# A decoder layer on one core: where TensorE waits for each part of an operand, three moved copies and transfers, and a shorter last offset

## The reference

```python
x = layernorm(x + attention(x))    # 32 query heads, 8 key/value heads of 128, causal, window 128
x = layernorm(x + cross(x, ctx))   # matmul(fake_quant(x), fake_quant(ctx)), 8 bits
x = layernorm(x + ffn(x))          # ternary weights, hidden size 2752
# attention: q, k, v = x @ wq.T, x @ wk.T, x @ wv.T; p = softmax(mask(q @ k.T / sqrt(128)))
#            (p @ v) @ wo.T, everything in fp32
# fake_quant(a): (clip(round(a / s + z), 0, 255) - z) * s
# ffn(x): gate, up = x / 128 @ wg.T, x / 128 @ wu.T; i = trunc(clip(silu(gate) * up * 128, -128, 127))
#         trunc(clip(i @ wd.T * 128, -128, 127)), as int8
# layernorm: (x - mean) / sqrt(var + 1e-5)
```

## Time and profile before

| | |
|---|---|
| median of 3 executions | 1465.61 us (1465.59 to 1466.85) |
| the profiled execution, its own time | 1466.88 us |
| its span in the trace | 1465.1 us |
| PE busy | 1429.0 us, 98% of the span |
| DVE, ACT, POOL busy | 68%, 53%, 51% |
| moved by DMA | 283.20 MB, 193 GB/s on the mean |
| mean granted clock of TensorE | 0.996 |

### The profile page before, as it was taken

One profiled execution on the slowest core, in us unless ns is written; L12 is line 12 of the kernel. 1 busy time (PEld: TensorE's weight loads), 2 busy tenths in 40 slices (PEclk: granted clock), 3 DMA queues, 4 the chain that ended last, 5 costly groups with the idle time before them and its releaser, 6 DMA issues.

```text
span 1465.1 us, 22782 instructions
## 1 busy us (share of the span) xinstructions
PE 1429.0 (98%) x7024; PEld 1153.3 (79%) x7024; DVE 999.4 (68%) x1768; ACT 782.7 (53%) x1553; POOL 740.7 (51%) x651
## 2 busy tenths in 40 slices
PE   8899999999999999999999999999989999999997
PEld 6688888888888888888888888887657888778643
DVE  7644444445656578888888888887786656566597
ACT  5433333333345466666575666565466555555674
POOL 0477777777565454555455555554476333433100
PEclk9999999999999999999999999999999999999998
DMA  6477877776663757675757676763151222222611
GB/s 230 146 271 283 286 281 270 273 275 256 212 239 108 282 180 277 200 267 179 265 196 271 206 265 209 269 236 127 41 181 74 94 100 81 76 93 86 230 43 74
DMA packets 114330, 283.20 MB, mean 193 GB/s; under 512 B 21216, under 2 KB 21600, under 8 KB 114272
## 3 DMA queue, kind: packets, MB, share of 16 engines
q1 hardware_dynamic: 114272, 282.50, 55.1%
HBM read 184.94 MB, written 95.42 MB: 191 GB/s over the span
## 4 chain that ended last, share of the span: by engine, by line
PE 50%; DVE 7%; ACT 4%; DMA 3%; issue 3%; POOL 2%; SPq 0%; DVEq 0%; ACTq 0%; POOLq 0%
PE ps L1141 7%; PE ps L1143 7%; PE ps L1142 7%; PE ps L1297 6%; PE ps L1298 5%; PE ps L1350 5%; PE ps L1070 2%; PE ps L1071 2%; PE ps L1072 2%; PE ps L1118 2%; PE ps L1117 1%; PE ps L1119 1%; PE ps L1083 1%; DVE u_val L2853 1%; PE ps L1222 1%
## 5 line engine op out<-in xcount | busy, mean ns | idle before, releaser
L1051 PE MATMUL ps<-xo_h,wb_h 128*128 128x512 f32 x644 | 251.6, 391 | 5.2 <-DVE xo_l L2391 2.0
L1053 PE MATMUL ps<-xo_h,wb_l 128*128 128x512 f32 x644 | 250.7, 389 | 0.0
L1052 PE MATMUL ps<-xo_l,wb_h 128*128 128x512 f32 x644 | 250.6, 389 | 0.0
L1141 PE MATMUL ps<-wo_h,o_h 128*128 128x512 f32 x512 | 207.9, 406 | 1.7 <-DMA wo_l<-wo_low 1.7
L1143 PE MATMUL ps<-wo_h,o_l 128*128 128x512 f32 x512 | 200.3, 391 | 0.0
L1142 PE MATMUL ps<-wo_l,o_h 128*128 128x512 f32 x512 | 200.1, 391 | 0.0
L2166 POOL TENSOR_TENSOR pm_l<-pt_l,upto 128x512 fp32r<-128x512 f32 x58 | 74.8, 1290 | 230.4 <-DVE pt_l L2490 230.4
L1517 ACT ACTIVATE wb_h<-wf_l 128x512 fp32r<-128x512 f32 x69 | 43.6, 632 | 197.7 <-DVE wf_l L2419 82.2
L1051 PEld LDWEIGHTS ps<-xo_h,wb_h 128*128 128x128 f32 x644 | 120.9, 188 | 33.2 <-issue 5.8
L1566 ACT ACTIVATE prob<-prob,exp_bias 128x128 f32<-128x128 f32 x256 | 99.8, 391 | 85.6 <-DVE exp_bias L2477 85.6
L2131 POOL TENSOR_TENSOR wb_l<-wf_l,wb_h 128x512 fp32r<-128x512 f32 x66 | 87.8, 1330 | 112.7 <-DVE s_sum L2414 56.8
(11 more groups left out here) (259 smaller groups left out, 3557.8 us busy)
## 6 DMA issues: line engine op xcount, KB each, us to landing
raw<-w_att SPq DMA_DIRECT2D x47, 512.0 KB, 5.4
f_raw<-w_gu SPq DMA_DIRECT2D x44, 512.0 KB, 5.0
u_gu<-f_unit SPq DMA_DIRECT2D x42, 512.0 KB, 4.9
gq<-u_gu SPq DMA_DIRECT2D x42, 512.0 KB, 3.9
wp_raw<-w_att SPq DMA_DIRECT2D x32, 512.0 KB, 5.8
wo_high<-wp_h SPq DMA_DIRECT2D x32, 512.0 KB, 2.8
wo_low<-wp_l SPq DMA_DIRECT2D x32, 512.0 KB, 4.1
q_rows<-c SPq DMA_DIRECT2D x64, 256.0 KB, 2.7
```

What stands on the lines that cost most here:

```text
L1051: pe.matmul(prod_ps[i], wh, chunk(xo_h[i], c), start=(i in OPENS and c == 0), stop=False, skip_group_check=True)
L1052: pe.matmul(prod_ps[i], wh, chunk(xo_l[i], c), start=False, stop=False, skip_group_check=True)
L1053: last = pe.matmul(prod_ps[i], wl, chunk(xo_h[i], c), start=False, stop=(c == KH - 1), skip_group_check=True)
L1141: pe.matmul(into, oh, wo_h[half][:, h, :], start=(h == 0), stop=False)
```

## The change

Four edits. First, in `plain_product` and `product` the three matmuls of a chunk go in another order: high x high, then the weight's low, then the low of x. The first waits for the highs (w_high, and x_high by chunk), the second once in a product for w_low, the third for x_low by chunk in quads 0 and 1. Second, on SP the second half of resid goes from slot 5 to slot 6 of the first group, behind the output weights. Third, on ACT the whole of a turned tile (xb_raw) is copied right behind its high part in the slots of tiles 1 to 3, and one saved half (early) before the scaling of a layernorm. Fourth, in the last tile DVE scales by a subtraction and a multiplication of two columns that are there one step sooner, so that the last step (the offset) is left out.

```diff
--- before.py
+++ after.py
@@ -825,10 +825,11 @@
                     load_out(g, 0)
                 if j == 6:
                     load_out(g, 1)
-                if first and j in (4, 5):
-                    sp.wait_ge(prod_done, last_product((PS1, PA22)[j - 4]))
-                    for tile in range((j - 4) * TPB, (j - 3) * TPB):
-                        sp.dma_start(resid[:, tile, :], x_rows[tile]).then_inc(x_loaded[j - 4], 16)
+                if first and j in (4, 6):
+                    part = (j - 4) // 2
+                    sp.wait_ge(prod_done, last_product((PS1, PA22)[part]))
+                    for tile in range(part * TPB, (part + 1) * TPB):
+                        sp.dma_start(resid[:, tile, :], x_rows[tile]).then_inc(x_loaded[part], 16)
                 if first and j == 7:
                     for i, source in ((S1, x1_scale), (Z1, x1_zp), (S2, x2_scale), (Z2, x2_zp)):
                         sp.dma_start(param(i), source.rearrange("(a b) -> a b", a=1).to_broadcast([P, 1])).then_inc(prm_loaded, 16)
@@ -1007,19 +1008,22 @@
             def plain_product(k, x_block, into, w, start, stop):
 
                 xh, xl = x_operand(x_block)
-                pe.wait_ge(w_low, block_count(0, w))
+                pe.wait_ge(w_high, block_count(0, w))
                 for c in range(KH):
-                    pe.wait_ge(x_low, x_count(x_block, c))
                     wh = wb_h[w][:, c * P:(c + 1) * P]
                     wl = wb_l[w][:, c * P:(c + 1) * P]
+                    pe.wait_ge(x_high, x_count(x_block, c))
                     pe.matmul(bank(into), wh, chunk(xh, c), start=(start and c == 0), stop=False)
-                    pe.matmul(bank(into), wh, chunk(xl, c), start=False, stop=False)
-                    last = pe.matmul(bank(into), wl, chunk(xh, c), start=False, stop=(stop and c == KH - 1))
+                    if c == 0:
+                        pe.wait_ge(w_low, block_count(0, w))
+                    pe.matmul(bank(into), wl, chunk(xh, c), start=False, stop=False)
+                    pe.wait_ge(x_low, x_count(x_block, c))
+                    last = pe.matmul(bank(into), wh, chunk(xl, c), start=False, stop=(stop and c == KH - 1))
                 last.then_inc(prod_done, 1)
 
             def product(n, i, opening=False):
 
-                pe.wait_ge(w_low, block_count(n, i))
+                pe.wait_ge(w_high, block_count(n, i))
                 if i == PA11:
                     pe.wait_ge(c1_done, 1 if opening else copy_count(n - 1, C_11) if isinstance(n, int) else n * 2 + 2)
                 if i == PS2:
@@ -1044,13 +1048,17 @@
                 if i == PS4:
                     pe.wait_ge(sums_done, corner_count(n, C_22))
                 for c in range(KH):
+                    wh = wb_h[i][:, c * P:(c + 1) * P]
+                    wl = wb_l[i][:, c * P:(c + 1) * P]
+                    if opening:
+                        pe.wait_ge(x_high, operand_count(i, c))
+                    pe.matmul(prod_ps[i], wh, chunk(xo_h[i], c), start=(i in OPENS and c == 0), stop=False, skip_group_check=True)
+                    if c == 0:
+                        pe.wait_ge(w_low, block_count(n, i))
+                    pe.matmul(prod_ps[i], wl, chunk(xo_h[i], c), start=False, stop=False, skip_group_check=True)
                     if opening:
                         pe.wait_ge(x_low, operand_count(i, c))
-                    wh = wb_h[i][:, c * P:(c + 1) * P]
-                    wl = wb_l[i][:, c * P:(c + 1) * P]
-                    pe.matmul(prod_ps[i], wh, chunk(xo_h[i], c), start=(i in OPENS and c == 0), stop=False, skip_group_check=True)
-                    pe.matmul(prod_ps[i], wh, chunk(xo_l[i], c), start=False, stop=False, skip_group_check=True)
-                    last = pe.matmul(prod_ps[i], wl, chunk(xo_h[i], c), start=False, stop=(c == KH - 1), skip_group_check=True)
+                    last = pe.matmul(prod_ps[i], wh, chunk(xo_l[i], c), start=False, stop=(c == KH - 1), skip_group_check=True)
                 last.then_inc(prod_done, 1)
 
             def scores(g, j):
@@ -1814,6 +1822,7 @@
                 if without_out:
                     if t < TPB:
                         left_high(t)
+                        left_whole(t)
                     elif i < TILES + 5:
                         right_high(t)
                 if i < TILES + 4:
@@ -1827,11 +1836,14 @@
                 if i < TILES + 1:
                     scale_rows(i - 1)
                 if t < TPB:
-                    left_whole(t)
+                    if not without_out:
+                        left_whole(t)
                     if i < TILES:
                         root(0, i)
                     normed(1, i - 4)
                     return
+                if i == TILES + 2:
+                    keep_early(0, 6)
                 if i < TILES + 4:
                     normed(1, i - 4)
                 mixed_high(t, T1L, T1H, 1, 1)
@@ -1842,7 +1854,6 @@
                     keep_early(4, 0)
                     act.activation(ln[:, 0, 21:22], ln[:, 0, 20:21], ACT.Silu)
                 if i == TILES + 2:
-                    keep_early(0, 6)
                     keep_early(1, 7)
                 if i == TILES + 4:
                     keep_early(2, 4)
@@ -3088,11 +3099,11 @@
                         unit_finish(t, half)
                     ln_variance(2, t)
                 t = TILES - 1
-                for i in range(5):
+                for i in range(4):
                     ln_link(2, t, i)
-                dve.wait_ge(ln_scale[2], TILES)
-                dve.tensor_scalar(rows2[:, t, :], rows2[:, t, :], ln_of(2, t)[:, 19:20], ln_of(2, t)[:, 20:21], ALU.mult,
-                                  ALU.add).then_inc(ln_done[2], 1)
+                dve.wait_ge(ln_step[2], (t + 1) * LN_STEPS)
+                dve.tensor_scalar(rows2[:, t, :], rows2[:, t, :], ln_of(2, t)[:, 12:13], ln_of(2, t)[:, 19:20], ALU.subtract,
+                                  ALU.mult).then_inc(ln_done[2], 1)
             with dve.Else():
                 for i in range(FIRST_SLOT, TILES + 6):
                     slot(i, True)
```

## The result

The changed kernel is slower: 1469.09 us in the median of 11 executions (1467.85 to 1471.02), against 1466.28 us for the kernel before (1465.12 to 1466.99) beside it. The medians lie 2.8 us apart. The forecast was 1465.4 us, no change, with a range up to 1467.4. The profiled execution took 1468.93 us, 2.05 more than the one before, and its span is 1467.2 us.

The account below looks back on a forecast made before the run. PE was taken to bound the kernel, busy 1429.0 of 1465.1 us. Terms -0.9 (opening), +1.0 (head slots), 0 (layernorm 2) and -0.25 (tail) sum to -0.15: 1465.4 us from the median of 1465.61, range 1462.5 to 1467.4.

Parts of the forecast that it names:

- rival (d): Steady projections: the added wait in each of 161 products is not hidden, +12.9 us, 1468.5 to 1478; chance 0.05.
- rival (e): Opening: the start gives nothing because a load of the first quads sets PE at 62.37; +0.75, 1466.4 us; chance 0.06.
- The stretch of layernorm 2: Turned rows: PE's waits for xb_raw and early go, but POOL and DVE set the pace; 0 us (ends 0, -0.5).
- The tail: Last tile: one DVE instruction of 0.21 us leaves the path that ends last; -0.25 us with its step.
- The mechanism of the head slots: Near 504 to 527 us: wo_l's 1.20 us stall goes, but prm, behind the moved 2 MB, lands 1.0 us later.
- The opening: Start of projections: high-first order starts PS4 and the copy c 0.91 us earlier; -0.9 us (ends -0.46, -1.0).
- Term two: Head slots, resid's second half moved: later prm delays PE's turn from 526.16 to 527.2; +1.0 us (ends 0, +1.75).
- rival (c): Head slots: the clock falls behind PE's idle time before 527.2, costing 1.5 us; +1.35, 1467.0 us; chance 0.13.
- its own condition: The clock fall decides once PE's idle time is as long as the 2.29 us seen; 3.2 us was forecast.

Follow-up runs that it names:

- second trace: The changed kernel run once more with nothing edited: 1469.69 us against 1466.92 for the kernel before, ratio 1.0013.
- the control: Changed kernel with PE's first pass through its loop over groups 1 to 6 written out, nothing else different: 1469.76 us, ratio 1.0025 to the kernel before.
- the fourteen traces above: All traces of these kernels; first to fifth DVE sum near layernorm 2 took 31.16 to 31.21 us, in eight with a clock fall as in six without.

## Why the prediction was wrong

**Right.** No added wait cost anything in the steady part, so rival (d) is out, and so is rival (e). The stretch of layernorm 2: 0 forecast and 0 measured, by the reason given (DVE waits for POOL). The tail: -0.25 both times. The mechanism of the head slots, too: wo_l's stall at 517.58 is gone, prm stands behind the 2 MB and is late.

**The opening, right with some luck in its size.** -0.9 was forecast, -0.99 measured, and -0.8 by itself. At the corner sum the trace is 1.20 us ahead, more than the end of -1.0 allowed, and the growing wait for the copy c takes 0.2 of it back, which the forecast had moving along in full. Single traces also differ here by as much as the term. PS4 starts at 51.24 to 51.97 us in the four traces with the old order and at 50.54 to 51.58 in the ten with the new one, 0.6 us earlier on the mean.

**Term two was mis-sized.** I took +1.0 within 0 and +1.75. It measures 0.81 + 0.97 = +1.78 at the turn. I had the reason, a queue that starts empty, and the bound of 1.75; I took the smaller value because I counted part of the 2.5 us of a lone load as something that both orders have. The window of 503 to 505 us shows a queue nearly idle for 2 us, at a share of 0.13. The upper end was the value to take, and over all traces it is even a little short. From the issue of the q_raw to the turn it is 20.3 to 21.3 us in five traces with resid in slot 5 and prm in slot 7, and 22.6 to 23.2 in five with resid moved and prm behind it, 2.1 more on the mean.

**The step that failed is the clock, which the sum put at nothing.** The fall of the clock behind PE's stall was rival (c), given 0.13, priced at 1.5 us from the one fall that the trace showed, and worked out at 1467.0. It measures 1.57 us in the changed kernel's trace, 2.03 in its second trace, 2.70 in the control, and 533.17 - 527.42 - 3.22 = 2.53 where resid moves alone. On the mean of the four that is 2.2 us, and the sum by it, -0.97 + 1.78 + 2.2 - 0.25 = 2.8, lies at what the medians show (1469.09 - 1466.28). It closes that well by chance, since its first two terms come from one pair of traces; with the means over all traces it is -0.6 + 2.1 + 2.2 - 0.25, about 3.4, still inside the interval of 1.3 to 3.7 us. The range ended at 1467.4, since it took (c) with one short fall and a part of term two's end; the two belong together, for a later prm makes the stall longer.

The weighing was wrong, not the list. The row for it stood there: 2.29 us of standing and then a clock of 0.50. The forecast itself said 3.2 us of standing before the turn, over the length from which (c) was said to decide. By its own condition (c) was more likely than not. The stall also came in two pieces with scores between, and it fell all the same. The price had the wrong source, though. The 1.5 us were read where the fall costs the layer nothing (the fourteen traces above); behind 527 us PE sets the pace, and there all that the slower matmuls lose is lost. What the Trainium skill says under "TensorE: Matmul & The Clock Gate", section "HAM oscillation — how this bites in real kernels", that long idle gaps close the gate, spoke for (c) and should have had its weight, though the waits in that section's own case are longer than those measured here. The traces agree in direction at this place, where the fall came behind 2.50 us in four of four; they do not agree as to length alone (last section). The rule of the Trainium skill, "DMA: Bandwidth & Descriptors", section "Rules for kernel authors", to issue early and wait late, was right for another load than the one that I applied it to. It is prm, which is tiny and has no condition: issued early it turns the changed kernel's ratio of 1.0013 into 0.9979.

**Open.** Why the fall at the same place is about twice as long in three traces (a mean clock of 0.83 over the 20 us) as in the first (0.91) was not tried.

## What to carry to other kernels

When a large load moves back in a queue, look at the smallest transfer that now stands behind it, and at whether the queue runs empty in the gap that the load leaves. Small loads without a condition belong ahead of the large ones. When a forecast makes one engine's idle time longer, price the clock at that place as a term of the sum and not as a remote case, and by who sets the pace behind it: where PE does, what the slower matmuls lose is lost, and where another engine does, the fall can cost nothing. A few redundant matmuls in the gap can show its price.

## What the runs showed that was not expected

The length of a stall does not settle alone whether the clock falls. Behind 1.69 us of waiting for wo_l it fell in the kernel with resid put back (PE's timeline, and the window behind it):

```profile
996.90 0.53 PE L1148 MATMUL ps<-wo_h,o_h 128*128 128x512 f32 x1 [1.69 <-DMA wo_l<-wo_low]
```

```profile
997.00:1001.00 4.00, 4.00 (x11) 3.14 (x12) 0.45 (x2) 1.65 (x8) 0.00 (x0) 0.57 0.39 158
```

It cost 1.60 us: from this matmul to a sum of DVE at 1051.76 it is 54.86 us, against 1049.92 - 996.66 = 53.26 before. But in the second trace of the changed kernel PE stood 1.90 us at the same matmul, and the clock did not fall.

Near 1072 us it is plainer still. With ACT's new order PE stands the same 2.16 us before the same product in ten traces (in three of them, this document's 2.56 and 2.39 among them, the first matmul is missing, so that the stall reads longer), and the clock fell in four and not in six. In the kernel with only ACT's moves the product then ran in 3.40 us for the 15 matmuls seen, at the full clock. So single traces of one kernel differ by a fall here and there, which was 1.6 to 2.7 us at 527 and 997 us and nothing near 1072, and a change of 2 us has to be read at its place in several traces, not from two spans.
